# GpSimd's row scatters placed ahead of the norms' powers in a fused attention and mixture-of-experts block

## What is computed

```
x = x + tanh(g_xattn) * xattn(layernorm(x), ctx, ctx)     # kp, vp = rope(ctx @ Wk.T), rope(ctx @ Wv.T)
x = x + tanh(g_ffn)   * ffn(layernorm(x))

gate_logits = einsum('ble,en->bln', x, gate_kernel)
top_k_weights, top_k_indices = top_k(gate_logits, 2)
softmax_probs = softmax(top_k_weights)
output = sum over the two chosen experts of
         softmax_prob * ((silu(x @ w0[e]) * (x @ w1[e])) @ wo[e])
```

## Time and profile before

| what | value |
|---|---|
| time, median of 3 runs | 670.18 us (670.08 to 670.79) |
| the profiled execution's own time | 668.73 us |
| its span in the trace | 666.9 us |
| PE, ACT, DVE, POOL busy share of the span | 84%, 65%, 59%, 57% |
| granted TensorE clock, mean over the span | 0.976 |
| attention's steady part, loop and what is around it | about 50 us to 370 us |

### The profile page before, as it was taken

The page is one execution under the profiler, slowest core; times in us unless marked ns, Lnnn a source line. Parts: engine busy times, 40 slices in busy tenths (PEclk is TensorE's granted clock), DMA queues, the critical chain, the costliest instruction groups (busy, mean ns, idle before and its releaser), DMA issues.

```text
span 666.9 us, 21070 instructions
## 1 busy us (share of the span) xinstructions
PE 560.3 (84%) x6123; PEld 466.8 (70%) x6124; DVE 394.7 (59%) x1418; ACT 431.2 (65%) x1090; POOL 382.3 (57%) x524
## 2 busy tenths in 40 slices
PE   8998898998988899899988878786777788888870
PEld 6886676776767677677766667775666677887770
DVE  6797787777777677677878543361232222223673
ACT  4897787887887788888777645342444446655650
POOL 3247756566575666657566365575555555554651
PEclk9999999999999999999999798997999999999995
DMA  3811111111111111111112112233222222225987
GB/s 82 241 27 53 46 35 55 39 51 44 42 49 36 55 40 47 48 33 58 41 59 58 33 49 65 72 97 96 85 76 68 75 73 78 73 71 162 279 260 224
DMA packets 64242, 52.98 MB, mean 79 GB/s; under 512 B 8607, under 2 KB 60064, under 8 KB 64176
## 3 DMA queue, kind: packets, MB, share of 16 engines
q1 hardware_dynamic: 46560, 30.79, 16.4%
q0 software_dynamic: 8448, 16.93, 7.7%
q10 hardware_dynamic: 9168, 4.46, 2.3%
HBM read 29.44 MB, written 23.22 MB: 79 GB/s over the span
## 4 chain that ended last, share of the span: by engine, by line
PE 53%; another core or an unknown queue 14%; ACT 10%; issue 10%; DVE 6%; ACTq 3%; DMA 2%; SPq 1%; POOL 1%; DVEq 0%; POOLq 0%
PE psK L583 11%; PE psH L603 6%; PE psH L483 6%; PE psH L489 5%; PE psG L498 4%; PE psH L498 3%; ACT wcur L757 3%; PE psK L471 3%; ACTq L319 3%; ACT hs L764 3%; ACT ys L771 3%; PE psO L476 2%; PE psK L619 2%; PE psO L518 2%
## 5 line engine op out<-in xcount | busy, mean ns | idle before, releaser
L1247 POOL DMA_INDIRECT results<-ys,zin x136 | 135.7, 998 | 107.2 <-ACT ys L771 69.8
L603 PE MATMUL psH<-zT,wcur 128*128 128x128 f32 (+1 forms) x760 | 135.4, 327 | 24.3 <-ACT wcur L757 15.0
L1174 POOL DMA_INDIRECT lists<-zp,dest x128 | 129.1, 1009 | 34.4 <-issue 31.1
L603 PEld LDWEIGHTS psH<-zT,wcur 128*128 128x128 f32 x760 | 110.8, 193 | 38.5 <-ACT wcur L757 19.0
L1077 DVE TENSOR_TENSOR hm<-psH,hs 128x512 f32<-128x512 f32 x68 | 47.0, 691 | 125.1 <-PE psH L603 35.8
L976 DVE TENSOR_REDUCE mx<-psH 128x8 fp32r<-128x512 f32 x128 | 82.4, 686 | 41.9 <-PE psH L483 28.1
L696 ACT ACTIVATE ex<-psH,rs 128x512 f32<-128x512 f32 x128 | 86.7, 687 | 25.9 <-PE psH L489 19.5
L583 PEld LDWEIGHTS psK<-v,pT 128*64 128x64 f32 x2048 | 70.4, 139 | 35.1 <-issue 34.1
L583 PE MATMUL psK<-v,pT 128*64 128x64 f32 x2048 | 82.1, 227 | 7.5 <-issue 7.1
L757 ACT COPY wcur<-w 128x512 f32 x95 | 56.1, 619 | 16.1 <-issue 13.7
L747 ACT COPY v<-kvr 64x64 f32<-64x64 f32 x256 | 63.7, 249 | 2.2
(11 more groups left out here) (176 smaller groups left out, 1153.0 us busy)
## 6 DMA issues: line engine op xcount, KB each, us to landing
yy<-results SPq DMA_DIRECT2D x16, 512.0 KB
zin<-lists SPq DMA_DIRECT2D x41, 130.0 KB
out_dram<-x ACTq DMA_DIRECT2D x16, 256.0 KB
xring<-in_x_dram SPq DMA_DIRECT2D x31, 128.0 KB
cring<-in_ctx_dram SPq DMA_DIRECT2D x31, 128.0 KB
zin<-lists SPq DMA_DIRECT2D x54, 65.0 KB
results<-ys,zin POOLq DMA_INDIRECT x136
w<-in_L_ffn_w_kernel_dram SPq DMA_DIRECT2D x2, 1024.0 KB, 7.2
```

The lines of the kernel that those rows point to most:

```text
L603: last = pe.matmul(bank[t.buf(2)][:, k * ET + c.start:k * ET + c.stop], wcur[:, t.buf(2), h, a, k * P:(k + 1) * P], zT[:, t.buf(2), c], st ...
L1174: nc.gpsimd.indirect_dma_start(lists, bass.IndirectOffsetOnAxis(ap=dest[:, t.buf(4), j:j + 1], axis=0), zp[:, t.buf(4), j, :], None).then_ ...
L1247: nc.gpsimd.indirect_dma_start(results, bass.IndirectOffsetOnAxis(ap=zin[:, t.buf(8), h, D:D + 1].bitcast(U32), axis=0), ys[:, t.buf(8), h ...
```

## The change

In GpSimd's attention step the call of `scatter` moves from behind `powers` and `counted` to in front of `powers`. Nothing else is edited; the other engines' programs are the same instruction for instruction.

```
                     if (t := ATT_POOL.at(s, -2)) and t.buf(4) == 3:
                         tokens(t)
+                    if t := ATT_POOL.at(s, -5):
+                        scatter(t, range(2))
                     if not static(s, NT - 1):
                         powers(ATT_POOL.at(s, 0), ATT_POOL.at(s, 3))
                     if (t := ATT_POOL.at(s, -2)) and t.buf(4) == 3:
                         counted(t)
-                    if t := ATT_POOL.at(s, -5):
-                        scatter(t, range(2))
                     if static(s, NT):
                         powers(ATT_POOL.at(s, -1), None)
```

## The result

The changed kernel takes 677.18 us (median; 676.17 to 678.71), the kernel before 670.13 us (669.59 to 670.79) in the same set of runs: ratio 1.0112, 95% interval 1.0089 to 1.0135. It is slower by 7.05 us where 10.9 were forecast. The profiled execution of the changed kernel was the longest of its runs, 678.71 us with a span of 676.9, so the traces lie 10.0 us apart, 3 more than the medians.

The account below looks back on a forecast made before the run. PE was taken as the bound, stalled by pairs across its step fronts. Steps of 5.8 + 4.8 + 7.2 + 6.5 = 24.3 us against 23.58, over 14.5 cycles, add 10.5 us: 681 us, range 662 to 700.

Parts of the forecast that it names:

- The mechanism of B and C: Steps B and C: B falls to 4.8 us, late `rs` lengthens C to 7.2; together 12.0 us against 11.5.
- The signs named: Changed profile: `ve` about 6.4 us into B, L696 about 3 us into C ended by `rs`, B near 4.8.
- A was summed at 5.8: Step A: its pair starts 0.8 us in, over the turns; a middle price of 1.0 gives 5.8 us.
- The sign named for D: Changed profile, step D: the pair close to L464, and DVE's L1000 waiting there as in A before.
- Step B, the wait: POOL in B: pair waits for `dest` until 3.94 us, `powers` ends 3.0 us later, C's exponentials about 2.0 us late.
- I count as covered: First 2 us of C: the pair's stall falls where PE waits for exponentials anyway; uncovered, up to 1.7 us more.
- Step D: Pair moves into POOL's gap ahead of `powers` and lies across D's front: price 0 to 1.7, D taken as 6.5 us.
- nearest to A's case: Pair at D's front: priced like the 6.52 us step A, so D takes 6.5 us.
- The text's other end: Pair at D's front: lowest price 0, from the 4.83 us step D of the earlier trace.
- Faster: Rival, 0.17: moving pairs off the fronts ends stalls; D and A 4.8 each, cycle 21.6, 641 us, or 656 with half.
- Worse stalls: Rival, 0.25: pairs cost full price in D and A, B and C keep theirs; 25.7 us a cycle, 701 us.
- Its second part: POOL in B: scatters meeting DVE's work take 2038 ns, not 969; `rs` 2.1 us later still; within the rival's 0.25.

Follow-up runs that it names:

- only_b: Kernel before with the scatters ahead of `powers` only in step B, step D left as it was: 684.92 us, ratio 1.031.
- b_split: Changed kernel, but only step B's first scatter stands ahead of `powers`, the second behind `counted`: 667.31 us, ratio 1.006 to the kernel before.
- fill kernels: Kernel before and changed kernel with each scatter replaced by a POOL memset of about 1 us: 590.97 and 609.31 us, one run each.
- b_wait_only: Kernel before, with POOL only waiting for the group's `dest` ahead of `powers` in step B, no scatter moved: 666.85 us, ratio 0.994.
- fill_after: Changed kernel's order with each scatter replaced by a POOL memset of about 1 us: 609.31 us, one run.
- only_d: Kernel before with the scatters ahead of `powers` only in step D, step B left as it was: 653.59 us, ratio 0.985; repeated, 0.990.
- after_again: The changed kernel unedited, in a further set of runs beside the kernel before: 676.03 us, ratio 1.011.
- combo: Kernel before with step D's scatters ahead of `powers`, and step B's `powers` waiting for `dest`: 560.72 us, ratio 1.019.

## Why the forecast held, and which of its terms did not

**What was right.** The mechanism of B and C. The signs named were `ve` about 6.4 us into B (6.85), L696 about 3 us into C ended by `rs` (3.58), B near 4.8 (4.85). only_b shows that this half carries the whole loss, b_split that it follows the lateness, and the fill kernels that it does so without any stall. A was summed at 5.8 and is 5.61. A's pair at 0.9 us is where the text had put it, and D's is close to D's front. The sign named for D did not come: DVE's L1000 starts at 255.48, 0.20 us after L518's end, with no wait.

**Step B, the wait, was short by half a microsecond, and C with it.** The text let the pair start when `dest` ends. In the trace 0.81 us lie between DVE's end at 244.99 and POOL's 245.80; in nine of the ten cycles up to 270 us it is 0.81 or 0.82, in the first 0.97. It belongs to the scatter and not to the wait: in b_wait_only `ve` waits for the same `dest` and starts 0.16 us after it (259.11 to 259.27). `dest` itself came 0.2 earlier than said, so the exponentials start 3.58 us into C and not 3.1. By the text's own sum C is then 4.81 + 3.58 - 0.74 = 7.65 us, against 7.2 forecast and 7.85 measured. The 0.2 that are left would be the part of the stall that "I count as covered"; in fill_after, without a stall, the sum goes the other way (L698 starts 2.49 us into its step, which gives 6.56, and takes 6.32), so the uncovered part may be some 0.4. No experiment measured it by itself.

**Step D was the wrong term: 6.5 was taken, 5.66 measured.** The range was right, 4.8 to 6.5, and the choice of the end "nearest to A's case" was not: the pair starts 0.4 us into D, not 0.1 before it as in A. In only_d some 0.3 us make that difference, 6.5 us with the pair at the front and 5.5 at 0.27 to 0.38; b_split's D shows that this is no rule for every neighbourhood. The text's other end, the D of 4.83 us, was one step: the eight of the table take 5.11 to 5.24. The two errors have opposite signs, and the cycle comes to 23.96 where 24.3 was said: 0.38 us more than before, not 0.7.

**The start was left out.** 14.5 x 0.38 is 5.5 us. The rest is at the start: from 52.08 to 91.86 the change costs 3.56 us, where the text's 0.7 a cycle gives about 1.1 for these 1.5 cycles. The stretch has two steps C, and both are long: 9.29 and 8.77 us, where they took 5.35 (from 52.14 to the 57.49 of the earlier trace rows) and 6.59 before. In the first ACT waits to 56.06 and DVE's maxima then to 60.00:

```profile
56.06 1.26 ACT L696 ACTIVATE ex<-psH,rs 128x512 f32<-128x512 f32 x2 [3.11 <-POOL rs L1202]
```

```profile
52.08:61.37 9.29, 6.68 (x76) 4.95 (x73) 5.00 (x18) 5.08 (x13) 8.30 (x11) 0.82 0.20 58
```

The lateness gives 4.81 + 3.98 - 0.74 = 8.05 us. The rest goes with the clock: it is granted at 0.82 here, in part 1.2 GHz, and PE is busy for 6.68 us, in the C of 246.09 for 5.92. after_again has the same two steps, 9.32 and 8.67 us at 0.82 and 0.80, so it is no accident of one trace. Part of it is won back in A and D.

The last stretch is another matter. Behind 283.55 the loss is 0.8 us a cycle (2.81 over 3.5 cycles), with steps C of 8.62 and 8.90 us at a granted clock of 0.84 and 0.81. In after_again these two have a clock of 1.00 and take 7.84 and 7.81, and the stretch loses 0.45 us in all:

```profile
283.60:366.08 82.48, 74.15 (x1022) 58.29 (x1018) 64.55 (x278) 65.62 (x173) 47.97 (x75) 1.00 0.15 43
```

So most of that loss is this execution's and not the change's. The steady part lost half of what was forecast, and a start that was in no term made up for much of it: that the total came out near is in part luck.

**The rivals.** "Faster" had the right idea in part: A's and B's stalls do shrink when the pairs leave their fronts, and only_d is that rival alone, 1.0 to 1.5% faster. Its condition was D's and A's pairs together under 2.3 us; they cost 5.66 + 5.61 - 2 x 4.81 = 1.65, so the condition was met. (The text's own terms give 23.58 - 4.8 - 7.2 - 9.6 = 1.98 for it and not 2.3; it was met either way.) It did not decide, because it was worked out with a C of 7.2: with 7.85 and a B of 4.85, the two pairs had to cost under 23.58 - 4.85 - 7.85 - 9.62 = 1.26. "Worse stalls" did not happen. Its second part, DVE holding up a scatter, did not either: the median of the 128 scatters is 972 ns and the longest 1237, where the line before had 969 and 2038. The rule of the Trainium skill (SBUF — State Buffer, Who interferes with whom) is not contradicted by that. The row that the prediction weighed it by couldn't test it: L986 has only one input in SBUF, since `psK` is in PSUM. L996 has both in SBUF. It takes 0.21 us as a rule, but 0.75 at 160.88 in the kernel before, where it starts inside a scatter that ends at 161.44, and 0.70 to 0.76 six times in only_b in the same way; many others that start inside a scatter keep 0.21. So where rows show a hold-up at all, it is DVE that is held and not the scatter.

**What stays open.** The path by which a scatter makes PE's results late, and why one set of runs was free of it. In such a condition the change was not measured. The fill kernels give an estimate: 1.49 us a cycle x 14.5 = 22 us, or the 18.3 us between their two times (one run each), since there would be no stall to win back; scatters make the exponentials later than memsets do, so it may be more.

## What to carry to other kernels

Before an instruction is moved ahead of another on an in-order engine, work out when its own latest operand comes: the wait is lent to everything behind it, and here the wait alone would have fitted into the slack, but with the two scatters behind it, it cost 1.1 us a cycle (only_b). Split such a move by the steps that it touches: one half was 3% slower and the other 1 to 1.5% faster. And where a price depends on where a transfer falls in another engine's step, compute that place to a tenth or two and test it, since the next transfer in the queue moves too.

## What the hardware showed

- While POOL issues a pair of scatters, PE's finished products are read late, by up to 1.6 us; with memsets in their place all four steps of the kernel before take 4.80 to 4.86 us. The price goes with the place: in the steady cycles pairs within 0.12 us of a step's first matmul go with steps of 6.4 to 6.8 us, and in the changed kernel and only_d those 0.27 to 0.9 us in with 5.5 to 5.7. It is not the place alone: b_split's D takes 6.3 to 6.7 us with its pair 0.85 to 0.95 us in, behind a scatter that ends at its front. The pair 3.4 us into C is followed by a D of 5.17 us in the mean (4.83 in the one of the earlier trace rows), where a step without any takes 4.81. With four scatters in a row DVE waits 2.89 us.
- The stall is not a matter of the program alone. The kernel before took 663.5 to 670.1 us in four sets of runs and 550.9 us in a fifth, the same instructions; in the fifth, kernels with scatters near the first products run steps of 4.80 us. The set of 550.9 and a set of 663.5 list the same chip. That condition is worth 113 to 119 us of this kernel, far more than any order of instructions won. Between the trace of the kernel before and combo's in the fifth set lie 108.2 us of span, and 64 of them behind the last L464 (307.9 against 243.7), most of it the experts' stage, which no experiment here looked into.
- POOL's scatter starts 0.81 us after the end of the DVE instruction it waits for; a memset or a `ve` that waits for the same one starts 0.15 to 0.16 us after it in most cycles.
- A stalled PE can be followed by a lower granted clock: 0.78 in the step after one with 1.44 us idle, and that step took 6.10 us without a scatter. It need not be: behind a step with 1.99 us idle the changed kernel kept 1.00.
